# The opening of a fused FFN and attention kernel: tile statistics moved, another bank for two results, routing steps and products interleaved anew

## The chip, the cores and the metric

The kernel runs on one core of a Trainium2 chip. The metric is the device time of one execution in microseconds (us), lower is better. Five engines work side by side and wait for each other by semaphores: TensorE (PE in the profile), VectorE (DVE), ScalarE (ACT), GpSimd (POOL) and SyncE (SP), which here issues all loads and stores. Each engine takes its own instructions strictly in the order in which they are written.

## The reference

x has shape (8, 1024, 128), 8192 tokens of width 128.

```
def ffn(x):                        # 16 experts of width 64, and a shared one
    scores = sigmoid(x @ gate_w.T)
    _, idx = top_k(scores + gate_b, 4)
    w = scores[idx]; w = w / sum(w) * 2.5
    comb = zeros(tokens, 16); comb[idx] = w
    y = sum over e of comb[:, e] * (silu(x @ w13_e gate) * (x @ w13_e up)) @ w2_e.T
    return y + (silu(gate_s) * up_s) @ w2_s.T
x = x + 0.5 * ffn(layernorm(x))
x = x + attention(layernorm(x))    # causal, rotated q and k, softmax
x = x + 0.5 * ffn(layernorm(x))
```

## The kernel before

The tokens are cut into 16 tiles of 512 (T = 0 to 15) for the first FFN, then 8 batches for attention, then 16 tiles for the second FFN. Only the opening is changed: the loads, the layernorm and routing of tiles 0 and 1, and the products of tile 0.

A product in full precision is three matmuls over a high and a low half (`mm3`, all recorded on line 1567). Per tile there are nine units: eight pairs of experts (j = 0 to 7) and the shared expert (j = 8). For a pair, TensorE makes a gate product into one of two gate banks (`G_BANK`, banks 0 and 1) and an up product; ScalarE applies silu; VectorE multiplies by the token's expert weights (`ffn_weighted`, lines 1146 for j below 4 of tile 0 and 1151 otherwise) and then by the up product (`ffn_h`, line 1161); ScalarE rounds that to a high half (`ffn_h_hi`, line 740), GpSimd subtracts to get the low half (line 518), and TensorE multiplies both by the second weights (`ffn_down`). A gate bank is free again when `ffn_weighted` has read it.

Routing: TensorE transposes the normalised tile (`ffn_xnT`, line 1654) and ScalarE and VectorE split it (`xh`, `xl`, line 1051). TensorE makes the router's logits in bank 7 (`T_BANK`), and VectorE takes 13 small steps, each counted in the semaphore `route_step`, from `ffn_logit0` (line 1064) to `ffn_comb` (line 1138). TensorE then transposes the result (`ffn_combT`, line 1671), ScalarE copies it to `combT` (line 740), and SyncE writes it to memory (line 389) and reads it back spread over the partitions: the expert weights of the tile for `ffn_weighted` (line 396) and two rows with mean and root (line 402, `rows<-comb_rows`). GpSimd needs those two rows to centre tile T + 2 (`ffn_center`, line 566), and does it between two low halves. For the first four pairs of tile 0 the weights don't take this way; they are spread by TensorE (`comb_spread`, line 1588).

The route of tile T + 1 is worked out during tile T. Layernorm statistics of a tile are four `bn_stats` (line 1179) and four `bn_aggr` (line 1188) on VectorE. For tile 2 they stand ahead of the first routing, for tile 3 between the first products of tile 0.

SyncE's order is written out: first all loads of the opening, then for each tile the store of `combT` and its reads. After those of tile 1 it issues the load of X for tile 5 and two tables of 1024 KB each, `cos` and `sin`; after them the result of tile 0 is stored and the `combT` of tile 2.

Of the kernel before, what the change touches and what calls it, by code (L numbers as in the profile page):

```python
# [91 lines left out]
def macaron(nc, x, x_t, w13T, w2T, wqkvT, gwT, gate_b, ident_d, mask_d, cos_d, sin_d, comb_d, x1_d, stat_d, out_t):  # L92
    x_v = x.rearrange("b (n p) d -> p (b n) d", p=P)

    with ExitStack() as ctx:
# [255 lines left out]
        def _(sp):  # L351
# [4 lines left out]
            load(X[:, 0:NB, :], x_v[:, 0:NB, :], x_loaded[0])  # L356
            load(ident[:], ident_d, gate_loaded)
# [148 lines left out]
        def _(pool):  # L506
# [61 lines left out]
            def ffn_tile(base, turn, c, first_batch=None):  # L568
# [7 lines left out]
                for j in range(UNITS):  # L576
                    g, k = (q + j) % 2, j % 3
# [13 lines left out]
                    if j < PAIRS:  # L591
                        low_half(h_l[k][:], h[g], h_h[k][:], h_lo_done)
                    else:
                        low_half(h_h[k][INTER:P, :], h[g][0:INTER, :], h_h[k][0:INTER, :], h_lo_done)
# [143 lines left out]
        def _(act):  # L738
# [43 lines left out]
            def ffn_combT(T, q):  # L782
                act.wait_ge(combT_ready, T + 1)
                wait(act, comb_written, 16 * (T - 1))
                copy(combT[q][:], bank[0:(NEXP + 2) * NB, T_BANK, 0:P]).then_inc(combT_done, 1)

            def ffn_silu(T, q, j):
# [4 lines left out]
                elif j < PAIRS:  # L792
                    nc.scalar.activation(bank[:, G_BANK[g], :], bank[:, G_BANK[g], :], ACT.Silu).then_inc(silu_done, 1)  # L793
# [32 lines left out]
            def ffn_tile(base, turn, c, first_batch=None):  # L826
# [7 lines left out]
                for j in range(UNITS):  # L834
# [5 lines left out]
                    if j == (7 if start else 6) and not last:  # L840
                        ffn_combT(T + 1, 1 - q)
                    if not start or j >= SPREAD:
                        ffn_silu(T, q, j)
                    if j == UNITS - 1 and ahead:
                        ffn_xh(T + 2, q, base)
                    if j >= (2 if start else 1):
# [3 lines left out]
                    if j == (3 if start else 2) and not last:  # L850
# [16 lines left out]
            def ffn(base):  # L867
                start = base == 0
                if start:
# [159 lines left out]
        def _(dve):  # L1029
# [112 lines left out]
            def ffn_weighted(T, q, j):  # L1142
# [8 lines left out]
                nc.vector.tensor_tensor(weighted[j % 2], bank[:, G_BANK[(q + j) % 2], :], comb_b[q][:, j, :],  # L1151
                                        ALU.mult).then_inc(weighted_done, 1)
# [51 lines left out]
            def ffn_tile(base, turn, c, first_batch=None):  # L1204
# [11 lines left out]
                if start:  # L1216
# [4 lines left out]
                    dve.wait_ge(x_loaded[3], 16)  # L1221
                    ffn_stats(L, Lx, 1 - q)
# [5 lines left out]
                    ffn_h(T, q, 2)  # L1228
                    ffn_logit0(N)
                    ffn_away0(N)  # L1230
                    ffn_logit(N)
                    ffn_weighted(T, q, 3)
                    ffn_recip(N)
                    ffn_h(T, q, 3)
                    ffn_score(N)
                    ffn_bias(N)
# [4 lines left out]
                    ffn_weighted(T, q, 4)  # L1241
                    ffn_mark(N)
                    ffn_h(T, q, 4)
                    ffn_weights(N)
                    for j in range(5, PAIRS):
# [78 lines left out]
            def ffn_start():  # L1324
# [5 lines left out]
                dve.wait_ge(gw_hi, 1)  # L1330
                low_half(gw_hl[:, NEXP:2 * NEXP], gw_f[:], gw_hl[:, 0:NEXP], gw_split)
# [3 lines left out]
                dve.wait_ge(x_loaded[1], 16)  # L1335
                ffn_stats(1, 1, 1)
                ffn_stats_wait(1)
                ffn_mv(1, 1)
                ffn_xl(0, 0)
                dve.wait_ge(x_loaded[2], 16)  # L1340
                ffn_stats(2, 2, 0)
# [223 lines left out]
        def _(pe):  # L1565
# [25 lines left out]
            def start_gate(j):  # L1591
# [3 lines left out]
                elif j >= SPREAD + 2:  # L1595
                    pe.wait_ge(weighted_done, j - 1)
                mm3(bank[:, G_BANK[j % 2], :], w13_h[:, 2 * j, :], w13_l[:, 2 * j, :], xh[0][:], xl[0][:]).then_inc(gate_ready, 1)
# [454 lines left out]
```

## Time and profile before

| | us |
|---|---|
| median of 3 runs | 843.43 |
| lowest, highest | 841.57, 843.57 |
| the profiled execution | 843.39 |
| its span in the profile | 841.6 |

The profiled execution took 1.8 us more than its span; it is within 0.1 us of the median. TensorE's granted clock was 1.00 of full speed over the whole span. TensorE was busy for 829.5 us, VectorE for 723.4, GpSimd for 612.7, ScalarE for 527.7. A timeline row gives the start, the length, the engine, the line and what was done; the bracket at its end says how long the engine had been idle and what ended that.

### The profile page before, as it was taken

What the parts mean: (1) busy time and instruction counts of PE and PEld (TensorE: products, weight loads), DVE (VectorE), ACT (ScalarE), POOL (GpSimd) and SP (SyncE); (2) the same over time, 40 slices, a digit from 0 to 9 for tenths busy, and PEclk for the clock granted to TensorE, in tenths of its full rate; (3) what the DMA queues carried; (4) which work ended last, traced back from release to release, by engine and by line L of the source; (5) the groups of instructions that cost most, each with busy time, mean ns of one, the idle gap of its engine ahead of it and who ended that gap; (6) DMA issues with size and microseconds to landing.
All of it is one profiled execution on the core that took longest, in us unless ns stands there. A gap on an engine that the chain in (4) does not pass through costs nothing.

```text
span 841.6 us, 16374 instructions
## 1 busy us (share of the span) xinstructions
PE 829.5 (99%) x4345; PEld 690.3 (82%) x4345; DVE 723.4 (86%) x2118; ACT 527.7 (63%) x1049; POOL 612.7 (73%) x559
## 2 busy tenths in 40 slices
PE   8899999999999999999999999999999999999998
PEld 7777888888888877888999999788888888888886
DVE  6989999989998988778887776899999999998886
ACT  5555666566665577676676666666656656666564
POOL 6776777777677678888888883567777777777664
PEclk9999999999999999999999999999999999999999
DMA  5777666666676533443333430566656555555553
GB/s 188 212 247 196 202 166 164 178 168 181 183 183 175 163 100 98 126 113 99 93 98 102 127 101 2 130 166 160 158 155 165 143 155 140 139 154 144 148 148 80
DMA packets 69377, 123.09 MB, mean 146 GB/s; under 512 B 8784, under 2 KB 19904, under 8 KB 69056
## 3 DMA queue, kind: packets, MB, share of 16 engines
q1 hardware_dynamic: 69312, 122.33, 53.8%
q8 instruction: 27, 0.44, 0.2%
q14 instruction: 38, 0.31, 0.1%
HBM read 104.28 MB, written 9.63 MB: 135 GB/s over the span
## 4 chain that ended last, share of the span: by engine, by line
PE 89%; DVE 4%; DMA 3%; ACT 1%; issue 1%; SPq 1%; DVEq 0%; ACTq 0%
PE bank L1567 84%; PE bank L1896 3%; DMA qkT<-comb_rows 1%; DMA comb_rows<-combT 1%; PE bank L1687 1%; DMA X<-in_x 1%; SPq L396 1%; PE bank L1679 1%; ACT probT L740 1%; PE bank L1671 0%; DVE probT L1161 0%; DVE prob L1151 0%; SPq L353 0%; DVE marked L1117 0%; DVE xl L1411 0%
## 5 line engine op out<-in xcount | busy, mean ns | idle before, releaser
L518 POOL TENSOR_TENSOR h_l<-probT,h_h 128x512 fp32r<-128x512 f32 x254 | 329.3, 1298 | 174.9 <-ACT h_h L740 174.4
L740 ACT ACTIVATE h_h<-probT 128x512 fp32r<-128x512 f32 (+1 forms) x286 | 179.5, 628 | 82.1 <-DVE probT L1161 79.0
L1567 PE MATMUL bank<-xh,w_h 128*128 128x512 f32 x544 | 220.4, 405 | 2.2 <-DVE prob L1151 1.7
L793 ACT ACTIVATE bank<-bank 128x512 f32<-128x512 f32 x252 | 146.8, 582 | 117.3 <-PE bank L1567 116.8
L1567 PE MATMUL bank<-xh,w_l 128*128 128x512 f32 x544 | 214.9, 395 | 0.0
L1567 PE MATMUL bank<-xl,w_h 128*128 128x512 f32 x544 | 214.7, 395 | 0.0
L1151 DVE TENSOR_TENSOR prob<-bank,qkT 128x512 f32<-128x512 f32 x252 | 172.8, 686 | 34.0 <-ACT bank L793 27.8
L1161 DVE TENSOR_TENSOR probT<-prob,bank 128x512 f32<-128x512 f32 x255 | 173.9, 682 | 17.7 <-POOL h_l L518 3.6
L1567 PEld LDWEIGHTS bank<-xh,w_h 128*128 128x128 f32 x544 | 102.2, 188 | 27.5 <-DVE probT L1161 3.3
L1567 PEld LDWEIGHTS bank<-xh,w_l 128*128 128x128 f32 x544 | 102.1, 188 | 23.8
L1567 PEld LDWEIGHTS bank<-xl,w_h 128*128 128x128 f32 x544 | 102.4, 188 | 21.1
L1567 PE MATMUL bank<-h_h,w_h 128*128 128x512 f32 x288 | 116.7, 405 | 0.3 <-DVE h_l L1031 0.2
L1567 PE MATMUL bank<-h_h,w_l 128*128 128x512 f32 x288 | 113.9, 396 | 0.2 <-ACT h_h L740 0.2
L1567 PE MATMUL bank<-h_l,w_h 128*128 128x512 f32 x256 | 101.0, 395 | 0.0
L1567 PE MATMUL bank<-stage,probT 128*128 128x128 f32 x576 | 77.1, 279 | 1.7 <-ACT probT L740 0.7
L740 ACT ACTIVATE probT<-bank 128x512 f32<-128x512 f32 (+2 forms) x96 | 45.2, 490 | 52.0 <-PE bank L1896 51.5
L1567 PEld LDWEIGHTS bank<-stage,probT 128*128 128x128 f32 x576 | 70.5, 191 | 7.7 <-ACT probT L740 2.6
L1567 PEld LDWEIGHTS bank<-h_h,w_h 128*128 128x128 f32 x288 | 54.2, 188 | 16.1 <-POOL h_l L518 1.4
L1567 PE MATMUL bank<-qkT 128*128 128x512 f32 (+3 forms) x288 | 66.4, 357 | 0.3 <-issue 0.3
L1567 PEld LDWEIGHTS bank<-h_h,w_l 128*128 128x128 f32 x288 | 54.2, 188 | 12.0 <-ACT h_h L740 0.6
L1567 PEld LDWEIGHTS bank<-h_l,w_h 128*128 128x128 f32 x256 | 48.1, 188 | 11.5 <-issue 0.2
L518 POOL TENSOR_TENSOR qkT<-rot,qkT 128x512 fp32r<-128x512 f32 x32 | 43.6, 1372 | 13.4 <-ACT qkT L740 11.7
(135 smaller groups left out, 1331.0 us busy)
## 6 DMA issues: line engine op xcount, KB each, us to landing
qkT<-comb_rows SPq DMA_DIRECT2D x190, 256.0 KB, 5.2
qkT<-comb_rows SPq DMA_DIRECT2D x124, 128.0 KB, 3.0
rows<-comb_rows SPq DMA_DIRECT2D x28, 512.0 KB, 7.1
stage<-stage SPq DMA_DIRECT2D x64, 128.0 KB, 2.7
X<-in_x SPq DMA_DIRECT2D x16, 256.0 KB, 7.3
stage<-in_x_t SPq DMA_DIRECT2D x16, 256.0 KB, 7.5
x_t<-stage SPq DMA_DIRECT2D x16, 256.0 KB, 2.1
out_x_t<-stage SPq DMA_DIRECT2D x15, 256.0 KB, 2.0
```

The costliest lines, as they stand in the source:

```text
L396: sp.dma_start(comb_b[q][a * INTER:(a + 1) * INTER, j0:j1, :], src[a:a + 1, j0:j1, :].to_broadcast([INTER, j1 - j0, TILE])).then_inc(comb_ ...
L518: nc.gpsimd.tensor_tensor(lo, f, hi.bitcast(F32), ALU.subtract).then_inc(done, 1)
L740: return nc.scalar.activation(dst, src, ACT.Copy)
L793: nc.scalar.activation(bank[:, G_BANK[g], :], bank[:, G_BANK[g], :], ACT.Silu).then_inc(silu_done, 1)
L1151: nc.vector.tensor_tensor(weighted[j % 2], bank[:, G_BANK[(q + j) % 2], :], comb_b[q][:, j, :], ALU.mult).then_inc(weighted_done, 1)
L1161: nc.vector.tensor_tensor(h_place(T, q, j), weighted[j % 2], bank[:, u, :], ALU.mult).then_inc(h_done, 1)
L1567: return nc.tensor.matmul(dst, lhsT, rhs, start=start, stop=stop)
L1679: ins = nc.tensor.transpose(bank[:, YT_BANK, n * P:(n + 1) * P], xT[c][:, n * P:(n + 1) * P], ident[:])
L1687: ins = nc.tensor.transpose(bank[:, m, n * P:(n + 1) * P], X[:, NB * Tx + n, :], ident[:])
L1896: ins = nc.tensor.transpose(bank[:, probT_bank(i, c, last), a * P:(a + 1) * P], prob[s][:, k0:k0 + P], ident[:])
```

## The change

Loads: X of tile 1 goes second, X of tiles 2 and 3 each ahead of the second and third part of w13.

VectorE: the statistics of tiles 1, 2 and 3 move into the start, ahead of the first routing. In tile 0, `ffn_weighted(3)`, `(4)` and `(5)` and their `ffn_h` stand earlier among the steps of the second routing.

Banks and places: h of tile 0 goes round three places instead of two (`rot[0]` is the third), `combT` of tile 0 is transposed into gate bank 0 instead of bank 7, and the seventh gate product (j = 6) goes into bank 4, where the last spread weights were.

TensorE and ScalarE: `ffn_xnT(1)` stands ahead of `ffn_combT(0)`, and the spread of pair 3 ahead of the logits of tile 1. `ffn_combT(1)` moves from unit 6 to unit 8 of tile 0, its copy on ScalarE from unit 7 to unit 8.

```diff
@@ h_place, g_bank
+            if isinstance(T, int) and T == 0 and j < PAIRS:
+                return (h[0], h[1], rot[0][:])[j % 3]
             return h[g]
+        def g_bank(T, q, j):
+            if isinstance(T, int) and T == 0 and j == SPREAD + 2:
+                return SPREAD_BANK[SPREAD - 1]
+            return G_BANK[(q + j) % 2]
@@ loads
             load(X[:, 0:NB, :], x_v[:, 0:NB, :], x_loaded[0])
+            load(X[:, NB:2 * NB, :], x_v[:, NB:2 * NB, :], x_loaded[1])
...
             load(w13_f[:, early[0], :], w13T[:, early[0], :], w13_loaded[0])
-            load(X[:, NB:2 * NB, :], x_v[:, NB:2 * NB, :], x_loaded[1])
+            load(X[:, 2 * NB:3 * NB, :], x_v[:, 2 * NB:3 * NB, :], x_loaded[2])
             load(w13_f[:, early[1], :], w13T[:, early[1], :], w13_loaded[1])
-            load(X[:, 2 * NB:3 * NB, :], x_v[:, 2 * NB:3 * NB, :], x_loaded[2])
+            load(X[:, 3 * NB:4 * NB, :], x_v[:, 3 * NB:4 * NB, :], x_loaded[3])
             load(w13_f[:, early[2], :], w13T[:, early[2], :], w13_loaded[2])
             load(w2_f, w2T, w2_loaded)
-            load(X[:, 3 * NB:4 * NB, :], x_v[:, 3 * NB:4 * NB, :], x_loaded[3])
@@ ScalarE
+                m = G_BANK[0] if isinstance(T, int) and T == 0 else T_BANK
+                copy(combT[q][:], bank[0:(NEXP + 2) * NB, m, 0:P]).then_inc(combT_done, 1)
...
-                    if j == (7 if start else 6) and not last:
+                    if j == (PAIRS if start else 6) and not last:
                         ffn_combT(T + 1, 1 - q)
...
+                    comb_spread(2)
                     ffn_combT(base, 0)
-                    comb_spread(2)
                     opening_xh(1, 1)
+                    ffn_h_hi(base, 0, 0)
                     ffn_silu(base, 0, 3)
-                    ffn_h_hi(base, 0, 0)
@@ VectorE, ffn_h
-                wait(dve, h_lo_done, UNITS * T + j - 1)
+                wait(dve, h_lo_done, j - 2 if isinstance(T, int) and T == 0 and j < PAIRS else UNITS * T + j - 1)
@@ VectorE, tile 0
-                    dve.wait_ge(x_loaded[3], 16)
-                    ffn_stats(L, Lx, 1 - q)
@@ TensorE, start_gate
-                elif j >= SPREAD + 2:
-                    pe.wait_ge(weighted_done, j - 1)
+                elif j == SPREAD + 2:
+                    pe.wait_ge(weighted_done, SPREAD)
+                elif j > SPREAD + 2:
+                    pe.wait_ge(weighted_done, SPREAD + 2)
+                if j == SPREAD:
+                    pe.wait_ge(combT_done, 1)
@@ TensorE, opening
+                ffn_xnT(1)
                 ffn_combT(0)
-                ffn_xnT(1)
...
+                comb_spread(3)
                 ffn_logits(1, 1)
-                comb_spread(3)
...
-                    if j == 6:
+                    if j == PAIRS:
                         ffn_combT(1)
```

VectorE in the start, before, from the statistics of tile 1 to the first logit step (`xl` is the low half of tile 0, TENSOR_REDUCE on `bank` is `ffn_logit0`):

```order
L1179 BN_STATS stats<-X 128x6 [waits x_loaded1]
L1179 BN_STATS stats<-X 128x6 x3
L1188 BN_AGGR mv<-stats 128x2 [waits stats_done]
L1188 BN_AGGR mv<-stats 128x2 x3
L1051 TENSOR_TENSOR xl<-bank,xh 128x512 [waits xh_done]
L1179 BN_STATS stats<-X 128x6 [waits x_loaded2]
L1179 BN_STATS stats<-X 128x6 x3
L1188 BN_AGGR mv<-stats 128x2 [waits first_var,first_xn,stats_done]
L1188 BN_AGGR mv<-stats 128x2 x3
L1064 TENSOR_REDUCE bank<-bank 128x64 [waits logits_ready]
```

The same stretch now, from the aggregation of tile 1 (its statistics stand further ahead):

```order
L1200 BN_AGGR mv<-stats 128x2 [waits stats_done]
L1200 BN_AGGR mv<-stats 128x2 x3
L1191 BN_STATS stats<-X 128x6 [waits mv_done,x_loaded2]
L1191 BN_STATS stats<-X 128x6 x3
L1043 TENSOR_TENSOR gw_hl<-gw_f,gw_hl 128x16 [waits gw_hi]
L1063 TENSOR_TENSOR xl<-bank,xh 128x512 [waits xh_done]
L1191 BN_STATS stats<-X 128x6 [waits mv_done,x_loaded3]
L1191 BN_STATS stats<-X 128x6 x3
L1200 BN_AGGR mv<-stats 128x2 [waits first_var,first_xn,stats_done]
L1200 BN_AGGR mv<-stats 128x2 x3
L1076 TENSOR_REDUCE bank<-bank 128x64 [waits logits_ready]
```

Tile 2's statistics have gone ahead of `xl`, and those of tile 3, which wait for `x_loaded3`, now stand between `xl` and the aggregation and first routing step.

VectorE in tile 0, before, during the second routing (`prob` rows are `ffn_weighted`, `probT` rows are `ffn_h`; the first two are pair 3):

```order
L1146 TENSOR_TENSOR prob<-bank,sin 128x512 [waits spread_ready,silu_done]
L1085 RECIPROCAL rlogit<-logit 128x64 [waits route_step]
L1161 TENSOR_TENSOR probT<-prob,bank 128x512 [waits up_ready,weighted_done,h_lo_done]
L1090 TENSOR_TENSOR bank<-bank,rlogit 128x64 [waits route_step,gsilu_done]
L1094 TENSOR_TENSOR biased<-bank,gb 128x4x16 [waits route_step]
L1104 MAX bank<-biased 128x8 [waits route_step]
L1104 MAX bank<-biased 128x8 x3
L1109 COPY take<-bank 128x4x4 [waits route_step]
L1151 TENSOR_TENSOR prob<-bank,qkT 128x512 [waits comb_loaded0_3,silu_done,route_step]
L1117 MATCH_REPLACE marked<-take,biased 128x20 x4
L1161 TENSOR_TENSOR probT<-prob,bank 128x512 [waits up_ready,weighted_done,h_lo_done]
```

The same place now; the first row is `ffn_h(3)`, `ffn_weighted(3)` stands ahead of these rows, and `rot` is the third place for h:

```order
L1173 TENSOR_TENSOR probT<-prob,bank 128x512 [waits up_ready,weighted_done,h_lo_done]
L1097 RECIPROCAL rlogit<-logit 128x64 [waits route_step]
L1163 TENSOR_TENSOR prob<-bank,qkT 128x512 [waits comb_loaded0_3,silu_done]
L1102 TENSOR_TENSOR bank<-bank,rlogit 128x64 [waits route_step,gsilu_done]
L1173 TENSOR_TENSOR probT<-prob,bank 128x512 [waits up_ready,weighted_done,h_lo_done]
L1106 TENSOR_TENSOR biased<-bank,gb 128x4x16 [waits route_step]
L1116 MAX bank<-biased 128x8 [waits route_step]
L1116 MAX bank<-biased 128x8 x3
L1121 COPY take<-bank 128x4x4 [waits route_step]
L1163 TENSOR_TENSOR prob<-bank,qkT 128x512 [waits comb_loaded0_3,silu_done,route_step]
L1129 MATCH_REPLACE marked<-take,biased 128x20 x4
L1173 TENSOR_TENSOR rot<-prob,bank 128x512 [waits up_ready,weighted_done,h_lo_done]
```

Two products more are done by the time of the marking step, and five instead of four stand between `ffn_logit0` and `ffn_comb` of tile 1.

TensorE after the first two spreads, before (`cos` holds the weights to be spread, `comb` the routing result, `xn` tile 1):

```order
L1671 MATMUL bank<-ident,comb 128x128 [waits neg_mean_done,rstd_done,route_step]
L1654 MATMUL bank<-ident,xn 128x128 [waits combT_done,xn_done]
L1654 MATMUL bank<-ident,xn 128x128 x3
L1588 MATMUL bank<-ident,cos 128x128 [waits weighted_done,spread_copied]
L1588 MATMUL bank<-ident,cos 128x128 x3
L1567 MATMUL bank<-xh,w_h 128x512 [waits h_done]
```

The same place now:

```order
L1674 MATMUL bank<-ident,xn 128x128 [waits route_step,xn_done]
L1674 MATMUL bank<-ident,xn 128x128 x3
L1695 MATMUL bank<-ident,comb 128x128 [waits neg_mean_done,silu_done,rstd_done,route_step]
L1604 MATMUL bank<-ident,cos 128x128 [waits weighted_done,spread_copied]
L1604 MATMUL bank<-ident,cos 128x128 x3
L1583 MATMUL bank<-xh,w_h 128x512 [waits h_done]
```

The transposes of tile 1 no longer wait for `combT_done`; the transpose of `comb` comes behind them and has a further wait for `silu_done`.

## Rows read from the trace of the kernel before

**Rows 1.** Page of the profile: busy time, share of the span, instructions.

```profile
PE 829.5 (99%) x4345; PEld 690.3 (82%) x4345; DVE 723.4 (86%) x2118; ACT 527.7 (63%) x1049; POOL 612.7 (73%) x559
```

**Rows 2.** Timeline, TensorE, 16 to 30 us: start, length, line, operation, count [idle, releaser].

```profile
16.23 1.32 PE L1588 MATMUL bank<-ident,cos 128*128 128x128 f32 x8 [0.84 <-DVE cos L1366]
...
18.12 0.63 PE L1654 MATMUL bank<-ident,xn 128*128 128x128 f32 x4 [0.45 <-ACT combT L740]
...
27.09 0.50 PE L1567 MATMUL bank<-xh,w_h 128*128 128x512 f32 x1 [1.68 <-DVE prob L1151]
...
29.19 0.33 PE L1671 MATMUL bank<-ident,comb 128*128 128x128 f32 x1 [0.43 <-DVE comb L1138]
```

**Rows 3.** Chain that ended last, 40 to 70 us: start, length, what.

```profile
48.94 5.17 DMA comb_rows<-combT
...
57.22 4.80 DMA qkT<-comb_rows
```

**Rows 4.** Timeline, VectorE, 53 to 64 us.

```profile
57.67 0.69 DVE L1151 TENSOR_TENSOR prob<-bank,qkT 128x512 f32<-128x512 f32 x1 [1.41 <-DMA qkT<-comb_rows]
```

**Rows 5.** Timeline, TensorE, transposes of line 1671 (second, third, fourth of them).

```profile
46.75 0.27 PE L1671 MATMUL bank<-ident,comb 128*128 128x128 f32 x1
...
67.52 0.30 PE L1671 MATMUL bank<-ident,comb 128*128 128x128 f32 x1
...
87.05 0.27 PE L1671 MATMUL bank<-ident,comb 128*128 128x128 f32 x1
```

**Rows 6.** Timeline, SyncE, 30 to 42 us.

```profile
31.32 0.32 SPq L389 DMA_DIRECT2D comb_rows<-combT  x1
...
40.99 0.43 SPq L353 DMA_DIRECT2D sin<-in_sin  x1
```

**Rows 7.** DMA issues at 40.99 us: count, KB each, us from issue to landing.

```profile
sin<-in_sin SPq DMA_DIRECT2D x1, 1024.0 KB, 11.5
```

**Rows 8.** Windows: length, busy by engine, granted clock, DMA share, GB/s.

```profile
32.00:34.00 2.00, 2.00 (x10) 1.61 (x9) 1.91 (x4) 1.11 (x2) 1.80 (x2) 1.00 0.08 18
38.00:51.00 13.00, 13.00 (x59) 10.50 (x59) 12.45 (x42) 7.34 (x15) 11.83 (x12) 1.00 1.03 320
```

**Rows 9.** Timeline, VectorE, 8 to 27 us.

```profile
8.55 0.69 DVE L1051 TENSOR_TENSOR xl<-bank,xh 128x512 fp32r<-128x512 f32 x1
10.08 0.87 DVE L1179 BATCH_NORM_STATS2 stats<-X 128x6 f32<-128x128 f32 x4 [0.83 <-DMA X<-in_x]
...
11.28 0.27 DVE L1064 TENSOR_REDUCE bank<-bank 128x64 f32<-128x128 f32 x1
...
22.83 0.30 DVE L1064 TENSOR_REDUCE bank<-bank 128x64 f32<-128x128 f32 x1 [0.27 <-PE bank L1567]
...
26.34 0.69 DVE L1151 TENSOR_TENSOR prob<-bank,qkT 128x512 f32<-128x512 f32 x1
```

**Rows 10.** Timeline, SyncE, 3 to 6 us.

```profile
3.70 0.50 SPq L353 DMA_DIRECT2D stage<-in_w13T  x1
...
4.72 0.51 SPq L353 DMA_DIRECT2D stage<-in_w13T  x1
...
5.75 0.43 SPq L353 DMA_DIRECT2D X<-in_x  x1
```

**Rows 11.** DMA issues at 3.70, 4.72 and 5.75 us, us to landing.

```profile
stage<-in_w13T SPq DMA_DIRECT2D x1, 256.0 KB, 4.5
...
stage<-in_w13T SPq DMA_DIRECT2D x1, 576.0 KB, 6.7
...
X<-in_x SPq DMA_DIRECT2D x1, 256.0 KB, 8.0
```

**Rows 12.** Timeline, ScalarE, copies into combT.

```profile
17.70 0.27 ACT L740 ACTIVATE combT<-bank 72x128 f32<-72x128 f32 x1 [0.26 <-PE bank L1671]
...
31.04 0.26 ACT L740 ACTIVATE combT<-bank 72x128 f32<-72x128 f32 x1
```

**Rows 13.** Timeline, GpSimd, 28 to 31 us.

```profile
29.37 1.31 POOL L566 TENSOR_TENSOR xn<-stage,rows 128x512 f32<-128x512 f32 x1 [2.12 <-DMA rows<-comb_rows]
```

More of the change, by code:

```diff
@@ L784, in ffn_combT @@
                 wait(act, comb_written, 16 * (T - 1))
-                copy(combT[q][:], bank[0:(NEXP + 2) * NB, T_BANK, 0:P]).then_inc(combT_done, 1)
+                m = G_BANK[0] if isinstance(T, int) and T == 0 else T_BANK
+                copy(combT[q][:], bank[0:(NEXP + 2) * NB, m, 0:P]).then_inc(combT_done, 1)
             def ffn_silu(T, q, j):
@@ L792, in ffn_silu @@
                 elif j < PAIRS:
-                    nc.scalar.activation(bank[:, G_BANK[g], :], bank[:, G_BANK[g], :], ACT.Silu).then_inc(silu_done, 1)
+                    G = bank[:, g_bank(T, q, j), :]
+                    nc.scalar.activation(G, G, ACT.Silu).then_inc(silu_done, 1)
                 else:
@@ L845, in ffn_tile @@
                         ffn_xh(T + 2, q, base)
+                    if start and j == SPREAD:
+                        ffn_gsilu(T + 1)
                     if j >= (2 if start else 1):
@@ L849, in ffn_tile @@
                         ffn_h_hi(T - 1, 1 - q, UNITS - 1)
-                    if j == (3 if start else 2) and not last:
+                    if j == 2 and not start and not last:
                         ffn_gsilu(T + 1)
@@ L1150, in ffn_weighted @@
                 dve.wait_ge(comb_loaded[q][comb_load(j)], 16 * (T - q) + 32 * (1 - skipped))
-                nc.vector.tensor_tensor(weighted[j % 2], bank[:, G_BANK[(q + j) % 2], :], comb_b[q][:, j, :],
+                nc.vector.tensor_tensor(weighted[j % 2], bank[:, g_bank(T, q, j), :], comb_b[q][:, j, :],
                                         ALU.mult).then_inc(weighted_done, 1)
@@ L1228, in ffn_tile @@
                     ffn_h(T, q, 2)
+                    ffn_weighted(T, q, 3)
                     ffn_logit0(N)
@@ L1240, in ffn_tile @@
                     ffn_taken(N)
-                    ffn_weighted(T, q, 4)
+                    ffn_weighted(T, q, 5)
                     ffn_mark(N)
-                    ffn_h(T, q, 4)
+                    ffn_h(T, q, 5)
                     ffn_weights(N)
-                    for j in range(5, PAIRS):
+                    for j in range(6, PAIRS):
                         ffn_weighted(T, q, j)
@@ L1334, in ffn_start @@
                     ln_apply(NB // 2, NB // 2 * a, first_xn, NB // 2 * a)
-                dve.wait_ge(x_loaded[1], 16)
-                ffn_stats(1, 1, 1)
                 ffn_stats_wait(1)
                 ffn_mv(1, 1)
+                dve.wait_ge(x_loaded[2], 16)
+                dve.wait_ge(mv_done, 1)
+                ffn_stats(2, 2, 0)
+                dve.wait_ge(gw_hi, 1)
+                low_half(gw_hl[:, NEXP:2 * NEXP], gw_f[:], gw_hl[:, 0:NEXP], gw_split)
                 ffn_xl(0, 0)
-                dve.wait_ge(x_loaded[2], 16)
-                ffn_stats(2, 2, 0)
+                dve.wait_ge(x_loaded[3], 16)
+                dve.wait_ge(mv_done, 2)
+                ffn_stats(3, 3, 1)
                 ffn_stats_wait(2)
@@ L1649, in ffn_xnT @@
                     pe.wait_ge(xn_done, opening_count(T) - 1)
-                wait(pe, combT_done, T)
+                wait(pe, route_step, ROUTE * T)
                 for n in range(NB):
@@ L1670, in ffn_combT @@
                     pe.wait_ge(neg_mean_done, pool_count(T + 2, base))
-                nc.tensor.transpose(bank[:, T_BANK, 0:P], comb[:].rearrange("p e n -> p (e n)"),
+                m = T_BANK
+                if isinstance(T, int) and T == 0:
+                    pe.wait_ge(silu_done, AHEAD)
+                    m = G_BANK[0]
+                nc.tensor.transpose(bank[:, m, 0:P], comb[:].rearrange("p e n -> p (e n)"),
                                     ident[:]).then_inc(combT_ready, 1)
```

17 lines of the change are left out of this document (9 added, 8 removed).

## The prediction

> **What bounds the kernel now.** I read the page first: TensorE is busy 99% of the span [rows 1], so only TensorE's waits, and what sets them, can be won. Then I read the timeline of TensorE in the opening. Once its products run, it waits four times: 0.84 us for the spread weights on VectorE, 0.45 us for the copy of combT on ScalarE, 1.68 us for the weighting of pair 4 on VectorE and 0.43 us for the last routing step, 3.40 us in all [rows 2]. The change can touch the last three, 2.56 us. That is 0.30% of 843.4, and 0.3% (2.5 us) is also about what a measurement here can tell from no change.
>
> Then I followed the chain of waits past the opening, and this decides my forecast. In the second tile the chain runs through TensorE. At 48.94 us it leaves TensorE: the store of tile 2's combT takes 5.17 us, and the last read that matters another 4.80 us [rows 3]. VectorE stands idle for 1.41 us at 57.67 until the expert weights of tile 2 have landed [rows 4]. TensorE feels it: from the second combT transpose to the third it takes 20.77 us, to the fourth 19.53 us [rows 5]. So tile 2 starts when its rows land, not when TensorE is ready, and whatever the opening gains is lost there unless these rows come earlier too.
>
> Why they land so late: SyncE stores tile 1's combT at 31.32, and all that it issues up to the table sin at 40.99 [rows 6] follows from this store without waiting for a compute engine. The sin table lands 11.5 us after its issue, at 52.5 [rows 7]. The DMA engines are nearly idle at 32 to 34 us (share 0.08) and full at 38 to 51 us (1.03) [rows 8]. The store of tile 2's combT is issued into this backlog and lands 1.6 us behind sin. The backlog starts with the store at 31.32. So to first order the whole kernel moves by as much as this store moves.
>
> **The change part by part.** The sum is the shift of that store.
>
> *Loads and statistics.* Before, the first step of the first routing starts 1.20 us after X of tile 2 has landed: 10.08 to 11.28 [rows 9], four bn_stats and four bn_aggr. Now statistics of tile 3 stand at this place, so it is 1.20 us after X of tile 3. Landings by slot: X of tile 2 takes the slot of the second w13 part, issued at 3.70 and landed 4.5 later, 8.2; X of tile 3 takes that of the third part, issued at 4.72 and landed 6.7 later, 11.4 [rows 10, 11]. The slot between them landed at 10.08. X of tile 3 has 256 KB where the third part had 576, so it needs 256/576 of the 1.3 us between 10.1 and 11.4: 10.7. The first routing then starts at 11.9, 0.6 late. Bounds: if both loads land before VectorE asks, only the logits are left. xl ends at 9.24 [rows 9], and eight small matmuls follow; eight transposes took 1.32 with a wait in them [rows 2], so I estimate 10.5, 0.8 early. If X of tile 3 keeps the full slot, 11.4 gives 12.6, 1.3 late. I take +0.6. Statistics of tile 2 ahead of xl also delay xl, to 8.2 + 0.87, about 9.2 (+0.6), but its logits are ready by 11.2 and this is covered by the wait for tile 3.
>
> The Trainium skill has a formula for this ("DMA: Bandwidth & Descriptors", Anatomy of one DMA): about 2.0 us plus bytes over 436 GB/s. With 1.65 MB up to and with X of tile 3, the formula puts it an estimated 5.8 us after the first load's issue, before 7 us; that is the early bound, and 843.2 in the sum. The trace disagrees: X of tile 2, at the end of 1.39 MB, would land 5.2 us after the first issue, and it landed at 10.08.
>
> *Third place for h, combT in gate bank 0.* The 0.45 us wait goes, because tile 1's transposes no longer wait for the copy: TensorE is then 0.15 late. The price: combT is transposed behind them (about 0.5 later, the 0.63 us row less what overlaps [rows 2]), and ScalarE copies it behind the copy for a spread; that costs up to half a us, as a copy of this size does by the nearest row, the product's 0.69 on VectorE. With the +0.6 above its copy, 17.70 before [rows 12], comes about 1.0 late, and so do tile 0's reads. GpSimd waits for the two rows at 29.37 already, for 2.12 us [rows 13]; that becomes 30.4, with low halves of pairs 4 and 5 queued behind and TensorE's down products waiting for these. The third place itself costs nothing: same instruction, SBUF as before, and it takes away a wait for a low half.
>
> *Statistics of tile 3 out of tile 0.* VectorE saves four bn_stats, 0.87 us [rows 9]. The logits of tile 1 don't gain: they come 0.15 late by TensorE's order and some 0.4 more behind the spread of pair 3, four transposes of which eight take 1.32 with a wait in them [rows 2]. First step of the second routing: 22.83 [rows 9] + 0.56, 23.4. VectorE has done one more product by then (up to 0.69) in place of the statistics.
>
> *Products between the steps.* Before, 22.83 to the transpose at 29.19 is 6.36 us with four products in it; now five, 0.69 more each [rows 2, 9]. Transpose possible at 23.4 + 6.36 + 0.69 = 30.4, +1.25. Below, if the fifth fits fully into gaps of dependent steps: +0.6; above, two: +1.9. In return the weighting of pair 4 and 5 comes early: the 1.68 us wait goes, and the seventh gate waits for pair 3 alone. But the eighth gate now waits for pair 5: 23.4 + 3.51 (22.83 to 26.34 before) + 0.69 + 0.7 = 28.3, where TensorE would be at 27.6: 27.09 less 1.68, 0.15 late, and three products of 0.7 us, the share of one in the 19.53 us that a tile of 26 takes [rows 5]. That is about 0.7 back. And the down product of pair 4 waits for GpSimd: 30.4 + 1.31 + 1.3 = 33.0, about 1.5 back. So of the 2.56 saved about 2.2 come back, and with the late start tile 1 begins some 0.3 to 0.6 late.
>
> *The store of tile 1's combT.* The copy comes 1.85 us after the transpose before (29.19 to 31.04) because it queues behind a high half; it queues behind the next high half now, so I keep the distance. Store: 31.32 + 1.25, about 32.6. Tile 2's rows land 1.2 late, and VectorE's wait of 1.41 grows to 2.0, for VectorE is ready at most 0.6 late. Sum: +1.2. The profiled execution took 843.39, the median is 843.43, so both give 844.6. With the bounds of the loads (-0.8 and +1.3 in place of +0.6) it is -0.2 to +1.9: 843.2 to 845.3.
>
> **The rivals.**
>
> A, the rows of tile 2 land as before. They are set by the drain of the tables, but a 36 KB store might overtake. For it: before, it landed only 1.6 us behind sin. Against: it was 5.17 us on the way. Then tile 2 starts at 57.67, VectorE is ready at 56.3 + 0.6, and the change is 0: 843.4. The Trainium skill says on the same page (Queues, rings and completion order) that completion isn't in the order of issue for one issuing engine; the landing behind sin shows no overtaking here.
>
> B, the waits that go are the gain: 2.56 less, and tile 2's rows come earlier too: 840.9. For it: VectorE loses 0.87 us of statistics in its fullest stretch, which ended the longest wait. Against: the store of combT must come earlier with two products moved ahead of the steps.
>
> C, slower: VectorE stands before X of tile 3 with the first routing behind it. Before, this load landed at 13.75 (issued 5.75, 8.0 later [rows 10, 11]). It passes two loads of 576 KB in the queue now, but if it lands at 12.0 or later, the first routing is 1.9 late and the store 2.6: 846.0. At its old 13.75 it would be 847.7. It decides from 12.0; against it stands the slot's 11.4.
>
> **How the numbers follow.** Forecast (+0.3 to +2.0): 0.59. A: 0.18. Early loads, 843.2: 0.06. B: 0.08, half of it beyond 0.3%, and C: 0.09, nearly all beyond. Faster by over 0.3% gets 0.05, slower 0.09, the same 0.86. Three runs of the same kernel lie 2 us apart, so the range takes 843.2 to 845.3 and over half a us on either side toward B and C: 841.9 to 846.0. The forecast alone would have 843.7 to 845.4, its +0.3 to +2.0.
>
> **What would show it.** X of tile 3 landing near 10.7 and VectorE idle before its statistics; the first logit step at 11.9; no 1.68 us wait on TensorE, but one before the eighth gate and one before the down product of pair 4, ended by VectorE and GpSimd; tile 1's combT stored near 32.6; the wait of 1.41 us grown to about 2. I am wrong if that store comes earlier than 31.3, or if it comes later and tile 2's rows do not.

## The result, and the profile of the changed kernel

| | before | changed |
|---|---|---|
| median, us | 842.67 (22 runs) | 843.48 (22 runs) |
| lowest, highest | 841.57, 844.12 | 842.43, 845.40 |
| ratio, 95% interval | | 1.0013 (1.0007 to 1.0019) |
| the profiled execution, us | 843.39 | 843.05 |
| a second one, taken later | 843.12 | 844.22 |

The changed kernel is slower by 0.13% going by the ratio and by 0.8 us going by the medians: within the 0.3% that counts as the same, on the side that was forecast. One profiled execution cannot show this. The first trace of the changed kernel comes from an execution faster than that of before, and the second, taken later, is 1.2 us longer than the first. So the readings below are of places, and where a place scatters both traces are given. One place carries the sum of the first FFN and none of the scatter of attention behind it: the last combT transpose of that FFN. It starts at 300.08 and 298.99 in the two traces of before and at 300.23 and 300.35 in those of the changed kernel, 0.75 us later in the mean.

The page's row of busy time, engine by engine: TensorE, VectorE and GpSimd do the same work as before [rows 1], to 0.2, 0.6 and 1.0 us.

```profile
PE 829.7 (99%) x4345; PEld 690.3 (82%) x4345; DVE 724.0 (86%) x2118; ACT 528.1 (63%) x1049; POOL 613.7 (73%) x559
```

TensorE's waits in the opening, from its timeline between 15 and 35 us (start, length, line, operation, [idle, releaser]), against [rows 2]:

```profile
16.20 1.32 PE L1604 MATMUL bank<-ident,cos 128*128 128x128 f32 x8 [0.57 <-DVE cos L1382]
...
28.11 0.50 PE L1583 MATMUL bank<-xh,w_h 128*128 128x512 f32 x1 [1.08 <-DVE prob L1163]
...
32.24 0.50 PE L1583 MATMUL bank<-h_h,w_h 128*128 128x512 f32 x1 [0.97 <-POOL h_l L526]
...
33.49 0.50 PE L1583 MATMUL bank<-h_h,w_h 128*128 128x512 f32 x1 [0.28 <-POOL h_l L526]
```

The waits of 0.45, 1.68 and 0.43 us are gone. In their place stand 1.08 us before the eighth gate and 0.97 and 0.28 us for low halves on GpSimd. All in all it is 2.90 us where it was 3.40. Of this half microsecond 0.27 is the first wait (0.84 to 0.57), which the prediction did not count as within reach and which was 0.70 in the second trace of before; the other three went from 2.56 to 2.33.

GpSimd's timeline at 28 to 32 us shows why the low halves are late. The two rows of tile 0 have come 0.27 later than in [rows 13], while GpSimd was idle sooner (from 26.5, for 27.3 before):

```profile
29.64 1.32 POOL L574 TENSOR_TENSOR xn<-stage,rows 128x512 f32<-128x512 f32 x1 [3.13 <-DMA rows<-comb_rows]
30.91 1.27 POOL L526 TENSOR_TENSOR h_l<-probT,h_h 128x512 fp32r<-128x512 f32 x1
```

VectorE's timeline at 8 to 30 us, for [rows 9]: the first step of the first routing (11.24) is where it was, and the last step of the second has moved.

```profile
8.79 0.68 DVE L1063 TENSOR_TENSOR xl<-bank,xh 128x512 fp32r<-128x512 f32 x1
10.17 0.87 DVE L1191 BATCH_NORM_STATS2 stats<-X 128x6 f32<-128x128 f32 x4 [0.70 <-DMA X<-in_x]
...
11.24 0.27 DVE L1076 TENSOR_REDUCE bank<-bank 128x64 f32<-128x128 f32 x1
...
22.78 0.30 DVE L1076 TENSOR_REDUCE bank<-bank 128x64 f32<-128x128 f32 x1
...
25.07 0.69 DVE L1163 TENSOR_TENSOR prob<-bank,qkT 128x512 f32<-128x512 f32 x1 [0.41 <-DMA qkT<-comb_rows]
...
29.88 0.27 DVE L1150 SCALAR_TENSOR_TENSOR comb<-bank,rsum 128x64 f32<-128x64 f32 x1
```

From 22.78 to 29.88 it is 7.10 us. Before it was 6.03, from the start at 22.83 [rows 9] to the last step, here in VectorE's timeline of the kernel before:

```profile
28.86 0.27 DVE L1138 SCALAR_TENSOR_TENSOR comb<-bank,rsum 128x64 f32<-128x64 f32 x1
```

It released TensorE at 29.19 [rows 2]. The rest of the chain, on ScalarE (against [rows 12]) and SyncE (against [rows 6]):

```profile
18.10 0.28 ACT L748 ACTIVATE combT<-bank 72x128 f32<-72x128 f32 x1
...
32.06 0.26 ACT L748 ACTIVATE combT<-bank 72x128 f32<-72x128 f32 x1
```

```profile
32.34 0.32 SPq L397 DMA_DIRECT2D comb_rows<-combT  x1
...
41.80 0.43 SPq L361 DMA_DIRECT2D sin<-in_sin  x1
...
49.39 0.33 SPq L397 DMA_DIRECT2D comb_rows<-combT  x1
54.85 3.69 SPq L404 DMA_DIRECT2D qkT<-comb_rows  x6
```

The store of tile 1 has moved from 31.32 to 32.34, and sin from 40.99 to 41.80. Then, in the chain of waits (for [rows 3]) and on VectorE (for [rows 4]):

```profile
49.39 5.45 DMA comb_rows<-combT
...
57.94 4.32 DMA qkT<-comb_rows
```

```profile
58.38 0.69 DVE L1163 TENSOR_TENSOR prob<-bank,qkT 128x512 f32<-128x512 f32 x1 [1.82 <-DMA qkT<-comb_rows]
...
62.35 0.69 DVE L1163 TENSOR_TENSOR prob<-bank,qkT 128x512 f32<-128x512 f32 x1 [0.18 <-DMA qkT<-comb_rows]
```

The wait has grown from 1.41 to 1.82 us, and the first product of tile 2 starts 0.71 later. TensorE's second, third and fourth combT transposes, for [rows 5]:

```profile
47.02 0.30 PE L1695 MATMUL bank<-ident,comb 128*128 128x128 f32 x1
...
67.78 0.30 PE L1695 MATMUL bank<-ident,comb 128*128 128x128 f32 x1
...
87.20 0.30 PE L1695 MATMUL bank<-ident,comb 128*128 128x128 f32 x1
```

Against [rows 5] the end of tile 1 is 0.27 late, and that of tile 2 still is, by 0.26. In before_again the same transposes stand at 47.03 and 66.58, so the first 0.27 is no more than scatter. The same two places in the second trace of the changed kernel, VectorE and then TensorE:

```profile
58.91 0.69 DVE L1163 TENSOR_TENSOR prob<-bank,qkT 128x512 f32<-128x512 f32 x1 [3.01 <-DMA qkT<-comb_rows]
```

```profile
46.36 0.27 PE L1695 MATMUL bank<-ident,comb 128*128 128x128 f32 x1
...
68.27 0.30 PE L1695 MATMUL bank<-ident,comb 128*128 128x128 f32 x1
```

Here tile 1 ends 0.39 early, and tile 2 still 0.75 late: TensorE came sooner and waited longer. In this trace tile 2 starts when its rows land, as the prediction read in [rows 5]; how far that held before the change is taken up at before_again below.

### The profile page after: what moved, and what is told of

It reads as the page before. It is cut to its first block, busy times and chain, and to the rows that moved or that the text cites. A ratio compares the mean times of both kernels' runs of the same rounds, so it can differ in the third digit from the quotient of the medians.

```text
span 841.2 us, 16377 instructions
## 1 busy us (share of the span) xinstructions
PE 829.7 (99%) x4345; PEld 690.3 (82%) x4345; DVE 724.0 (86%) x2118; ACT 528.1 (63%) x1049; POOL 613.7 (73%) x559
## 4 chain that ended last, share of the span: by engine, by line
PE 89%; DMA 4%; DVE 2%; SPq 2%; ACT 1%; issue 1%; POOL 0%; DVEq 0%; ACTq 0%; POOLq 0%
PE bank L1583 83%; PE bank L1920 3%; DMA qkT<-comb_rows 1%; DMA comb_rows<-combT 1%; SPq L404 1%; DMA rows<-comb_rows 1%; PE bank L1711 1%; PE bank L1703 1%; DMA X<-in_x 1%; ACT probT L748 1%; PE bank L1695 0%; SPq L361 0%; DVE probT L1173 0%; POOL h_l L526 0%; DMA stage<-stage 0%
```

## The experiments

Kernels timed on the same chip share its runs of before. Each kernel has 11 or 12 runs, e1 5 and changed 22; the ratio with its interval is an estimate of its own and not the quotient of the two medians, from which it differs most in e2 (0.9997, the quotient is 0.9989). "Store to reads" is the time from SyncE's store of tile 1's combT to its first read of tile 2's expert weights, which is issued as soon as tile 2's store has landed. The last column but one is VectorE's wait for these weights, the last the time between TensorE's second and third combT transposes.

| kernel | median / before, us | ratio (95%) | store at | store to reads | wait | tile |
|---|---|---|---|---|---|---|
| before | | | 31.32 | 22.81 | 1.41 | 20.77 |
| before_again | one execution, 843.12 | | 31.15 | 22.48 | 0.59 | 19.55 |
| changed | 843.48 / 842.67 | 1.0013 | 32.34 | 22.51 | 1.82 | 20.76 |
| changed_again | 843.87 / 842.43 | 1.0015 (1.0006, 1.0024) | 32.09 | 23.23 | 3.01 | 21.91 |
| e1_copy_late | 845.38 / 842.80 | 1.0034 (1.0021, 1.0047) | 33.97 | 22.51 | 2.01 | 21.04 |
| e4_front_only | 842.44 / 842.80 | 0.9996 (0.9987, 1.0005) | 31.03 | 22.44 | 1.16 | 19.91 |
| e5_back_only | 843.63 / 842.80 | 1.0014 (1.0006, 1.0023) | 32.10 | 22.51 | 1.80 | 21.09 |
| e6_copy_early | 842.84 / 842.43 | 1.0009 (0.9998, 1.0019) | 31.90 | 22.41 | 1.43 | 20.28 |
| e8_order_only | 845.35 / 842.78 | 1.0031 (1.0022, 1.0039) | 32.25 | 22.50 | none | 19.62 |
| e9_comb_first | 843.99 / 842.78 | 1.0012 (1.0003, 1.0021) | 32.20 | 23.35 | 2.63 | 21.88 |
| e2_tables_apart | 841.89 / 842.80 | 0.9997 (0.9989, 1.0006) | 31.44 | 21.06 | none | 19.37 |
| e3_changed_tables_apart | 841.93 / 842.43 | 0.9995 (0.9986, 1.0004) | 31.83 | 18.65 | none | 19.37 |
| e7_front_tables_apart | 841.80 / 842.43 | 0.9988 (0.9980, 0.9997) | 30.89 | 19.36 | none | 19.36 |
| e10_three | 841.91 / 842.78 | 0.9987 (0.9978, 0.9996) | 31.28 | 18.95 | none | 19.39 |

**Is it the store? e1_copy_late** is the kernel before with the copy of tile 1's combT, and so its store, moved back.

```diff
-                    if j == (7 if start else 6) and not last:
+                    if j == (PAIRS if start else 6) and not last:
                         ffn_combT(T + 1, 1 - q)
```

> The kernel before with one edit: ScalarE copies tile 1's combT at unit 8 of tile 0 instead of unit 7, behind the high half of pair 6 and so about 2.0 us later (31.04 to about 33.1). Nothing else moves. Theory (the store of tile 1's combT sets when tile 2's rows land): the store goes from 31.32 to about 33.3, tile 2's first rows land 1.4 to 2.0 us later, the wait of 1.41 us at 57.67 grows to about 3, and the time grows by 1.2 to 2.0 us. Rival A (the rows of tile 2 land as before): the wait stays 1.4, the time within 0.3 us. Rival B (waits of the opening decide): TensorE has no new wait there, so 0.

It came out 2.6 us slower, and the reads of tile 2 began at 56.48 instead of 54.13. So a late store costs, and rival A, by which tile 2's rows land as before, is out. It cost more than I expected: the move was larger (33.97 for 31.32), and the weights of tile 1 itself now came late too, while the wait of tile 2 grew to 2.0 and not to 3, as VectorE's timeline in this kernel shows:

```profile
39.09 0.69 DVE L1151 TENSOR_TENSOR prob<-bank,qkT 128x512 f32<-128x512 f32 x1 [1.16 <-DMA qkT<-comb_rows]
...
60.03 0.69 DVE L1151 TENSOR_TENSOR prob<-bank,qkT 128x512 f32<-128x512 f32 x1 [2.01 <-DMA qkT<-comb_rows]
```

TensorE makes the second combT transpose at 48.48 here, where it was 46.75 and 47.03 before: 1.5 to 1.7 of the 2.6 us are lost in tile 1, ahead of tile 2's rows. So e1 shows that this store costs, but not that all of its cost goes through tile 2.

**Is it the tables? e2_tables_apart and e3_changed_tables_apart** load cos and sin not behind tile 1's reads but behind those of tiles 10 and 11, in the kernel before and in the changed one. Attention, which uses them, starts behind tile 15.

```diff
-                load(cos[:], cos_d, rope_loaded)
-                load(sin[:], sin_d, rope_loaded)
...
+                    if T == 10:
+                        load(cos[:], cos_d, rope_loaded)
+                    if T == 11:
+                        load(sin[:], sin_d, rope_loaded)
```

> The kernel before, with the loads of the cos and sin tables (1024 KB each) taken from behind tile 1's reads and put behind those of tile 10 and of tile 11, one each. Theory: the store of tile 2's combT meets no backlog and lands in about 1.5 us instead of 5.2, VectorE's wait of 1.41 us at the start of tile 2 goes, the third combT transpose follows the second by 19.4 us instead of 20.8, and if one table in a tile is hidden the time falls by 1.2 to 1.6 us. Rival: the tables cost the same where they stand now, two waits of half the size, and the time stays within 0.3 us.

> The changed kernel with the two tables behind tiles 10 and 11, as in e2. Theory: tile 2 no longer waits for its rows, so what is left is the opening itself, in which TensorE's waits are 2.9 us in all in the changed kernel (0.57, 1.08, 0.97, 0.28) against 3.4 before; third combT transpose 1.2 to 1.9 us earlier than in the kernel before, time 1.0 to 1.8 us below it, within 0.4 us of e2. Rival (the opening costs by itself, whatever tile 2 does): still 0.8 us above e2.

The wait of tile 2 is gone in both, and the tile takes 19.37 us. SyncE's timeline in the changed kernel with the tables apart: the store of tile 2 is followed by its reads 1.7 us after its issue instead of 5.46.

```profile
48.75 0.32 SPq L397 DMA_DIRECT2D comb_rows<-combT  x1
50.48 6.29 SPq L404 DMA_DIRECT2D qkT<-comb_rows  x10
```

Behind tiles 10 and 11 the tables cost nothing: tiles 10 to 12 take 19.35 or 19.36 us in both traces, so the rival of e2 falls. And the two kernels, 0.13% apart with the tables behind tile 1, are alike without them as far as the runs can tell: 0.9995 against 0.9997, each give or take 0.0009, medians 841.93 and 841.89 on two chips. The last combT transpose of the first FFN is at 298.17 in the changed kernel and at 298.63 in the one before, so the 0.75 us of loss seen there is gone as well. So the loss goes through these tables. Both times missed what I expected. The kernel before was to gain 1.2 to 1.6 us and gained 0.9 by the medians; its interval, from 0.9 us less to 0.5 more, holds no change too. The tile of 1.4 us more was of one execution, and before_again waited only 0.59. The changed kernel was to end 1.0 to 1.8 us below the kernel before and ended 0.5 below it; but against itself with the tables behind tile 1 it gained 1.9 us, 843.87 against 841.93 on the same chip, by intervals that don't meet. Whether the tables hold the store up by standing ahead of it in the queue or by filling the DMA engines, these runs don't separate: moving them takes both away.

**Which part? e4_front_only** is the kernel before with the new loads and the early statistics; **e5_back_only** is the changed kernel with the old ones. Their edits are the hunks "loads" and, on VectorE, the statistics of the diff above, applied alone and taken back.

```diff
+                dve.wait_ge(x_loaded[1], 16)
+                ffn_stats(1, 1, 1)
...
                 ffn_xl(0, 0)
+                dve.wait_ge(x_loaded[3], 16)
+                dve.wait_ge(mv_done, 2)
+                ffn_stats(3, 3, 1)
```

> The kernel before with the first part of the change alone: the new order of the loads and the statistics of tiles 1, 2 and 3 ahead of the first routing. The trace of the changed kernel has its first routing at 11.24 against 11.28, so nothing is lost there. Theory: VectorE has 0.87 us less in tile 0, the logits of tile 1 still come at 22.8 by TensorE, so the second routing ends at most 0.1 to 0.3 earlier, the store of combT comes at 31.0 to 31.3, and the time is 0 to 0.3 us less. Rival B (VectorE's load in the opening decides): 0.9 us less.

> The changed kernel with loads and statistics as in the kernel before; the places, banks and the order of products, routing steps and combT as changed. Theory: the one product more between the steps and the later logits move the store of tile 1's combT to 32.4 to 33.2, as late as in the changed kernel or up to 0.8 later, since the statistics of tile 3 are back in VectorE's stretch; the time is 0.2 to 1.2 us more than before. Rival B: the 1.68 us wait is gone here too, and the time is over 1 us less.

The back part alone costs what the whole change costs, 1.0014 for 1.0013, with the store at 32.10, a little ahead of the range expected. The front part alone is not a cost: the store comes 0.29 earlier (and at 30.89 in e7, which has the same opening, where three executions of the opening of before have 31.15 to 31.44), and the time is 0.36 us less by the medians, which its interval doesn't tell from none. My sum had put +0.6 of its +1.2 on this part. VectorE loses the 0.87 us of statistics in its full stretch there, and TensorE's wait for pair 4 stays what it was, 1.67 (TensorE's timeline):

```profile
26.80 0.51 PE L1569 MATMUL bank<-xh,w_h 128*128 128x512 f32 x1 [1.67 <-DVE prob L1151]
```

So that wait is not a matter of VectorE's load (the argument for rival B). The order has a part in it: pair 4's weighting stood behind the steps, and with the new order alone (e8) the wait is 1.09.

**Can the gain be kept? e6_copy_early** is the changed kernel with tile 1's combT copied one unit earlier, behind the silu of the eighth gate.

```diff
-                    if j == (PAIRS if start else 6) and not last:
+                    if j == 6 and not start and not last:
                         ffn_combT(T + 1, 1 - q)
...
+                    if j == PAIRS - 1 and start:
+                        ffn_combT(T + 1, 1 - q)
```

> The changed kernel with one edit: ScalarE copies tile 1's combT at unit 7, behind silu of pair 7 and ahead of the high half of pair 6, instead of at unit 8. TensorE's transpose ends at 31.3, so the copy comes at 31.4 instead of 32.06, and the store at 31.7 instead of 32.34. Theory: tile 2's rows land 0.3 to 0.6 us earlier than in the changed kernel and the time is 0.3 to 0.6 us less, so +0.2 to +0.5 against the kernel before. Rival: the store is not what counts, and the time is that of the changed kernel.

In its execution the opening ran 0.4 later from the first transpose on, and the store still came 0.44 earlier than in the first trace of the changed kernel. The median is 1.0 us below changed_again on the same chip, where 0.3 to 0.6 were expected; the intervals of the two ratios overlap, so this is likely and not shown.

**e7_front_tables_apart** puts the edits of e4 and e2 together.

> The kernel before with two things: loads and statistics of the change (as e4) and the two tables behind tiles 10 and 11 (as e2). Theory: the two add only in part, since e4 gained through tile 2's rows landing sooner and e2 takes that wait away; what remains of e4 is what TensorE's start of tile 1 gains, 0 to 0.4 us. Time 1.2 to 1.8 us below before, 0 to 0.4 below e2. Rival: they add in full, 2.2 or more.

It is faster than before by 0.12%, with an interval below 1, but by 0.6 us going by the medians, half of the least that I had expected (1.2 to 1.8).

**changed_again** is the changed kernel, unedited.

> The changed kernel once more, beside the others on one chip. Both theories: 0.4 to 1.2 us over the kernel before, as measured; its trace shows whether the landing of tile 2's rows (58.38 in the first trace) and the stretch behind it come out the same again.

It repeats the loss, 1.0015, and gave the second trace read above.

**e8_order_only** is the kernel before with nothing but VectorE's new order in tile 0.

```diff
+                    ffn_weighted(T, q, 3)
...
-                    ffn_weighted(T, q, 3)
-                    ffn_recip(N)
...
+                    ffn_recip(N)
+                    ffn_weighted(T, q, 4)
+                    ffn_h(T, q, 4)
...
-                    ffn_weighted(T, q, 4)
+                    ffn_weighted(T, q, 5)
...
-                    ffn_h(T, q, 4)
+                    ffn_h(T, q, 5)
```

> The kernel before with VectorE's new order of products and routing steps in tile 0 alone; places, banks, loads, statistics and combT as before. Theory: one product more stands between the first step of the second routing and its last, so from 22.83 to 28.86 becomes 6.03 + 0.69 (0 to 0.4 more if pair 4 waits for its rows); the store of tile 1's combT comes 0.6 to 1.1 later, VectorE's wait at tile 2 grows, the time is 0.4 to 1.0 us more. TensorE's wait of 1.68 us gets shorter by some 0.7 and this is not seen in the time. Rival B: that wait is what counts, and the time is 0.5 us less.

I was wrong by a factor: 2.6 us. In this kernel TensorE still has the transpose of tile 1's result at unit 6, ahead of products that are ready. TensorE's timeline:

```profile
25.91 0.50 PE L1569 MATMUL bank<-xh,w_h 128*128 128x512 f32 x1 [1.09 <-DVE prob L1151]
...
30.31 0.33 PE L1673 MATMUL bank<-ident,comb 128*128 128x128 f32 x1 [2.75 <-DVE comb L1138]
```

It waits 2.75 us there, for 0.43 before. The result is as late in the changed kernel (29.88 and 29.98), but the transpose has moved two units back, behind products that are ready, and waits for nothing (there is none at 31.00). So that edit is probably what makes the order affordable, but no run has it alone: e5, at 1.0014, differs from e8 in banks and places too. My working had no term for it, neither in the prediction nor here. The profiled execution of e8 took 843.30, the fastest of its twelve, so why its typical one takes 2 us longer this trace doesn't show: the 2.75 us are seen, but a 2.6 us loss and the trace of a loss of 0.5 don't fit into one account.

**e9_comb_first** is the changed kernel with tile 0's combT transposed and copied ahead of the transposes of tile 1, still in gate bank 0.

```diff
+                ffn_combT(0)
                 ffn_xnT(1)
-                ffn_combT(0)
```

> The changed kernel with the transpose of tile 0's combT ahead of tile 1's transposes again, and its copy ahead of the copy for a spread; it stays in gate bank 0, so tile 1's transposes don't wait for the copy. Theory: tile 0's rows land 0.3 to 0.5 earlier than in the changed kernel, VectorE's wait of 0.41 us for them ahead of pair 4 goes, GpSimd's 3.13 us wait gets 0.4 shorter, the store of tile 1's combT comes at about 31.9 instead of 32.34, and the time is 0.2 to 0.5 us less than the changed kernel's. Rival: no difference.

That missed. (In the row below `sin` holds the spread weights; the table comes later.) VectorE's wait of 0.41 for the weights of pair 4 goes, but now pair 3's spread comes late, and VectorE's timeline shows a wait for it:

```profile
22.47 0.69 DVE L1158 TENSOR_TENSOR prob<-bank,sin 128x512 f32<-128x512 f32 x1 [0.76 <-PE bank L1604]
23.19 0.30 DVE L1076 TENSOR_REDUCE bank<-bank 128x64 f32<-128x128 f32 x1
...
29.74 0.27 DVE L1150 SCALAR_TENSOR_TENSOR comb<-bank,rsum 128x64 f32<-128x64 f32 x1
```

The first step starts 0.41 later (23.19 for 22.78), and the last comes at 29.74: what one wait gave the other took.

**e10_three** is the changed kernel with the edits of e3, e6 and e9.

> The changed kernel with three edits: the two tables behind tiles 10 and 11 (as e3), tile 1's combT copied at unit 7 (as e6), tile 0's combT transposed and copied first (as e9). Theory: once the tables are away tile 2 waits for nothing, so the two earlier stores bring only what GpSimd's rows and VectorE's pair 4 gain in tile 0, 0.2 to 0.5 us over e3; 1.0 to 1.5 us under the kernel before. Rival: the edits add in full, 1.0 under e3.

It is 0.13% faster than before, as expected, and nothing under e3 by the medians (841.91 for 841.93), where 0.2 to 0.5 us were expected. It and e7 are the two kernels whose interval lies below 1. TensorE waits 2.11 us in its opening, the least of all.

**before_again** is the kernel before, in one further execution.

> The kernel before once more, for a second trace. Theory: the wait for tile 2's rows is there again, 1.2 to 2.0 us, and from the second combT transpose to the third it takes 20.5 us or more. If it is absent, the chain read from the first trace was an accident of that execution.

That missed: its wait at tile 2 was 0.59 us, for 1.2 or more, and its tile 19.55 us long, for 20.5 or more. By the test that I had set, the long tile 2 of [rows 5] was an accident of that execution: before the change, the rows of tile 2 held TensorE up for about 1.4 us in one execution and for about 0.2 in the other (the tile takes 19.37 with the tables away). In the traces of the changed kernel it is 1.4 and 2.5 us. The time of before_again was 0.3 us lower only: stretches that the change doesn't touch scatter as much. From the last combT transpose of the first FFN to the first of the second, across attention, it took 226.39 us here and 225.65 in the first trace; over all kernels it was 225.35 to 227.21.

## Why the prediction was right, and where its terms were off

**The step that decided held for the landing, and in part for the time.** "To first order the whole kernel moves by as much as this store moves": in the eight kernels with the tables behind tile 1 the store lies between 31.03 and 33.97, and the reads of tile 2 begin 22.41 to 22.81 later in eight of ten traces, 23.23 and 23.35 in two. So the reads follow the store nearly one to one, over 2.9 us. The load of sin shows the same: issued 40.62 in before_again and 40.99 before, 41.54 and 41.80 in the changed kernel; landed at 52.1, 52.5, 54.4 and 53.8. The reads of tile 2 begin 0.9 to 1.6 us behind it each time. The Trainium skill has a rule that fits ("DMA: Bandwidth & Descriptors", Queues, rings and completion order): data writes may pass each other, but a DMA's semaphore increment lands only after every earlier write of that DMA engine. By that rule tile 2's store, 36 KB, can't report before what stands ahead of it on each DMA engine has been written. The traces agree: 4.1 to 6.7 us with the tables ahead, 1.7 to 3.3 without. They would look the same if the store only had to wait its turn, and no run here tells the two apart.

That the whole kernel moves with the store is shown less well. Three executions of the opening of before (both of its traces and e2) have the store at 31.32, 31.15 and 31.44, three of the changed opening (with e3) at 32.34, 32.09 and 31.83: 0.8 us later in the mean, which is what the medians lost. Store and median go together in six of the seven kernels edited with the tables in place, from -0.29 and -0.36 us in e4 to +2.65 and +2.6 in e1. In e8 they don't: 0.93 later, 2.6 slower, and no wait at tile 2 in its trace. And tile 2 did not wait for its rows in every execution of the kernel before, as before_again shows.

**The size: +1.2 forecast, +0.8 measured.** The forecast was 844.6 and the median 843.48. Of the 1.1 us between them 0.76 is the base: three runs had put the kernel before at 843.43, 22 runs put it at 842.67. So the time itself came out where rival A had it (843.4), and only the difference from before, and the traces, speak for the forecast. Two terms of the store's shift were off, in opposite directions; that they nearly cancel is luck.

- *Loads and statistics, +0.6: measured +0.0.* This was mis-sized. X of tile 3 landed at 10.1, not 10.7, and X of tile 2 at 7.3, not 8.2; VectorE's statistics start at 10.17 where those of tile 2 started at 10.08. I had treated landings as slots and added a share of the time between two of them. They don't add: before, X of tile 2 landed 1.9 behind the w13 part ahead of it (8.2 to 10.1), now X of tile 3 lands 0.7 behind its own (issued 4.25, 5.1 on the way, 9.4), with 256 KB more ahead of it in the queue. The formula quoted in the prediction from the Trainium skill ("DMA: Bandwidth & Descriptors", Anatomy of one DMA), which put this load before 7 us, is off by three the other way; the page fits it to one transfer issued by GpSimd, not to a row of them issued by SyncE. The place scatters besides: the first logit step starts at 11.24 and 10.64 in the changed kernel, and between 10.39 (e1) and 11.43 (e2) in the opening of before.
- *Second routing, +0.69: measured +1.07.* The product more cost 0.66, close to what was worked out. The other 0.41 is a wait that I had put at nothing: pair 4's weighting now stands so early that the rows of tile 0 have not landed (25.07, [0.41 <-DMA]). It is 0.29 in changed_again and 0.16 in e3, and the stretch 6.99 and 6.85. The logits of tile 1, which I had at +0.56, were not late at all (22.78 for 22.83); that is the loads' term once more, for the 0.56 is +0.6 for the loads, -0.45 for the wait that goes and +0.4 for the spread, and without the first it is nearly nothing.
- *Their sum, the store's shift, +1.25: measured +1.02* in the first trace (7.10 less 6.03, and a start 0.05 earlier), +0.77 in the second.

**The wait of tile 2.** It was to grow from 1.41 to 2.0, and was 1.82 and 3.01, against 1.41 and 0.59 before. What I had not seen is that the third product of the tile has its own wait: 62.35 for 62.11 before, so in the first trace a start 0.71 late ends 0.26 late. The time gained between is slack of VectorE, not of the DMA.

**The small sums.** combT of tile 0 is copied 0.40 late, not 1.0, 0.6 of which was the loads' term; so GpSimd has the rows at 29.64 and not 30.4, and the down products wait 0.97 + 0.28 for the forecast 1.5. The eighth gate waits 1.08 for the forecast 0.7, probably by the 0.41 above. Of 2.56 us saved 2.33 come back there, against the forecast 2.2.

**The rivals.** A falls by e1 and by the second trace. B falls: the waits went, and the gain did not come, although 0.5 us less is waited for. C's load landed at 10.1, far from 12.0. What stays open is the loss of e8, and the scatter of one execution against another in the length of tile 2 (19.55 and 20.77 in the same kernel), which is larger than the effect; the ratios over many runs carry the verdict, not the traces.

## What to carry to other kernels

A wait that goes can be worth nothing ahead of a point that a chain of transfers paces: find which issue starts that chain and ask what the edit does to it. Work put between the steps of a result that others need is paid by that result's lateness, and an engine that takes the result in the order of its program must have it later in that order too, or it waits there. Large loads that nobody needs soon don't belong ahead of a small store on whose landing reads wait: moving two of them left no difference that the runs can tell between two kernels that lay 0.13% apart, and made the changed one 1.9 us faster.

## What the runs showed of the hardware

- A store of 36 KB took 4.1 (e4) to 6.7 us (changed_again) until the read behind it could be issued when two loads of 1024 KB stood ahead, and 1.5 (tile 1 of before, 31.32 to 32.80) to 3.3 (tile 2 of e2, 49.22 to 52.50) where they did not.
- The same program's tile 2 took 19.55 us in one execution and 20.77 in another, and attention 225.65 and 226.39, with the granted clock at 1.00 in both. From the second combT transpose of the second FFN to its last it took 270.44 to 270.47 us in every trace; from the first, with the tile behind attention, 285.15 to 286.39.
- In six of the fourteen traces, all with the tables behind tile 1, a tile of the steady part took 19.33 us instead of 19.36: over 12 tiles 0.3 us. No edit alone brings it: the changed kernel had one of each.
